# Expert layers that fetch token rows by indirect reads and send results by indirect writes

## What is computed

```python
probs = softmax(x2 @ wr)                       # x2: normalized tokens
gate_v, gate_i = top_k(probs, TOP_K)
pos = place of the token among those that chose the same expert
keep = pos < C
buf[ef, posc] = tok * keep                     # one block of C rows per expert
h = gelu(einsum('ech,ehf->ecf', buf, w1) + b1)
y = einsum('ecf,efh->ech', h, w2) + b2
out = x + sum over choices of y[ef, posc] * gate * keep
```

| layer | experts | choices per token | rows per expert | hidden width |
|---|---|---|---|---|
| A (L0) | 64 | 2 | 78 at most | 256 |
| B (L2) | 8 | 1 | no limit, in blocks of 250 | 512 |
| C (L3) | 8 | 2 | 250 at most | 256 |

## Time and profile before

### The profile page before, as it was taken

The page is one execution under the profiler, slowest core; times in us unless marked ns, Lnnn a source line. Parts: engine busy times, 40 slices in busy tenths (PEclk is TensorE's granted clock), DMA queues, the critical chain, the costliest instruction groups (busy, mean ns, idle before and its releaser), DMA issues. The chain is left out here.

```text
span 3491.5 us, 42084 instructions
## 1 busy us (share of the span) xinstructions
PE 2712.7 (78%) x12559; PEld 1905.1 (55%) x12560; DVE 1672.9 (48%) x3338; ACT 944.3 (27%) x2087; POOL 245.7 (7%) x247
## 2 busy tenths in 40 slices
PE   5888869967999872999488599946868589998554
PEld 3555546446878642666265266645635367775442
DVE  6777742154888532443433632231132378884323
ACT  1222230112777610111111122211111247774100
POOL 0000000000000103111200000010010000000123
PEclk9999989988999875999698799958979789998576
DMA  7000060211000015997323120014341100000354
GB/s 250 24 0 0 0 170 2 57 42 29 18 21 14 16 33 185 305 314 257 99 51 122 38 58 12 1 66 156 107 102 27 52 25 22 21 15 8 84 165 119
DMA packets 133922, 269.43 MB, mean 77 GB/s; under 512 B 44950, under 2 KB 46182, under 8 KB 132539
## 3 DMA queue, kind: packets, MB, share of 16 engines
q10 hardware_dynamic: 53198, 116.25, 11.2%
q1 hardware_dynamic: 51245, 106.69, 10.0%
q0 software_dynamic: 29376, 45.16, 4.3%
HBM read 189.78 MB, written 73.05 MB: 75 GB/s over the span
## 5 line engine op out<-in xcount | busy, mean ns | idle before, releaser
L1042 DVE TENSOR_REDUCE mx<-ps 125x1 f32<-125x500 f32 (+1 forms) x480 | 274.3, 589 | 57.6 <-PE ps L812 41.0
L243 PE MATMUL ps<-onehot_src,onehot_dst 125*128 x1200 | 258.7, 354 | 42.2 <-DVE onehot_dst L219 17.5
L937 ACT ACTIVATE probs_hi<-ps 125x500 fp32r<-125x500 f32 (+1 forms) x480 | 255.4, 532 | 125.5 <-DVE probs_lo L994 81.1
L218 DVE TENSOR_SCALAR onehot_src<-iota,src_f 125x1250 f16 x400 | 217.6, 544 | 112.4 <-PE ps L243 100.0
L939 ACT ACTIVATE x<-ps 125x500 f32<-125x500 f32 (+1 forms) x480 | 258.7, 539 | 0.0
L994 DVE TENSOR_TENSOR probs_lo<-x,probs_hi 125x1250 fp32r<-125x1250 f32 x160 | 240.9, 1506 | 34.9 <-ACT x L939 31.4
L1525 DVE COPY yb<-ps 78x512 f32<-78x512 f32 (+1 forms) x100 | 68.7, 688 | 349.4 <-PE ps L1462 220.9
L1462 PE MATMUL ps<-w2s,hT 128*78 128x512 f32 (+1 forms) x480 | 217.1, 599 | 2.7 <-ACT hT L1487 2.6
L243 PEld LDWEIGHTS ps<-onehot_src,onehot_dst 125*128 x1200 | 120.8, 102 | 173.6 <-issue 119.7
L1487 ACT ACTIVATE hT<-ps,b1s 128x78 f32<-128x78 f32 (+1 forms) x240 | 66.6, 342 | 519.7 <-PE ps L1453 495.9
L812 PE MATMUL ps<-K_hi_lo,Q_hi_twice 128*125 128x500 f32 (+1 forms) x480 | 182.5, 386 | 22.2 <-DVE mx L1042 16.9
(11 more groups left out here) (346 smaller groups left out, 4869.2 us busy)
## 6 DMA issues: line engine op xcount, KB each, us to landing
room<-in_L_ffn_w_p ACTq DMA_DIRECT2D x72, 512.0 KB, 7.1
w2s<-in_L_ffn_w ACTq DMA_DIRECT2D x72, 512.0 KB, 7.3
buf<-zeros SPq DMA_DIRECT2D x37, 512.0 KB
G<-c_spill ACTq DMA_DIRECT2D x2, 5859.4 KB
xb<-buf SPq DMA_DIRECT2D x64, 156.0 KB
yb<-yb POOLq DMA_DIRECT2D x64, 156.0 KB, 7.0
xb<-buf SPq DMA_DIRECT2D x36, 250.0 KB
tv<-in_L_ffn_tv_W_p SPq DMA_DIRECT2D x2, 4096.0 KB
```

Of the source, the lines that this page charges most:

```text
L218: v.tensor_scalar(ohs[:, slot, :].rearrange("p o n -> p (o n)"), io16[:, 0:N], sF[:, bass.ds(tile, 1)], None, ALU.is_equal)
L243: mm_ = pe.matmul(ps[:, 3 * half + c, 0:cn], ohd[:, slot, :].rearrange("p o n -> p (o n)"), ohs[:, slot, c0:c0 + cn].rearrange("p o n -> p ...
L937: act.activation(PH[:, t % 2, c0:c0 + cn], ps[0:P, ST + n, 0:cn], ACT.Exp, scale=SCALE).then_inc(p_hi, 1)
L1042: v.tensor_reduce(mx[:, t, n:n + 1], ps[0:P, SQ + cc % 2, 0:cn], AX.X, ALU.max)\
```

## The change

Routing now forms, for each slot of each unit, the number of the token that fills it (`take`) and the row to which its result goes (`give`, numbered by choice and token; unused slots read token 0 and write to spare rows). It does so with one-hot matrices and one chain of products on PE. In the same block SP writes the normalized token rows, dense, to HBM, and ACT issues all first-layer biases and the weights of the first three groups. In `experts` POOL gathers the rows of each unit by indirect DMAs and scatters its results by indirect DMAs; SP's loop of loads is gone. In A and C `xb` and `yb` hold two units (`DEEP`); in B one. The second bias and the residual are added to `x` at the start of `experts`. `combine` loads the results with direct DMAs from SP and ACT, in five parts, and in A and B takes the row statistics that the next stage needs. The start of the program fills fewer rows of HBM with zeros. The diff, cut to its core (of `combine`, `program` and the table of `route` only added lines; layer A takes the branch `NB == E_`):

```diff
--- before.py
+++ after.py
+            @block.sync
+            def _(sp):
+                for to, what in in_two(rowtiles(r.rows_dram), rows_in):
+                    sp.dma_start(to, what).then_inc(r.rows_out, 16)
+                sp.wait_ge(r.rows_out, 32)
...
+                for n in range(topk * T):
+                    c, t = n // T, n % T
+                    pe.wait_ge(hots, 2 * c + 2)
+                    mm = pe.matmul(ps[0:R, 1, 0:NB], rowhot[:, c, t, :], unithot[:, c, t, :], start=(n == 0),
+                                   stop=(n == topk * T - 1))
+                mm.then_inc(slots_done, 1)
...
+                if early is not None:
+                    early(act)
...
+                def rows_of_slots(c, row):
+                    v.tensor_tensor(rowhot[:, c, :, :], ioR[:, :].unsqueeze(1).broadcast_to([P, T, R]),
+                                    row.unsqueeze(2).broadcast_to([P, T, R]), ALU.is_equal).then_inc(hots, 1)
+                def units_of_slots(c, out, hot, number):
+                    return v.tensor_tensor(out, hot, number.unsqueeze(2).broadcast_to([P, T, hot.shape[2]]), ALU.mult)
...
+                    if NB == E_:
+                        for c in range(2):
+                            rows_of_slots(c, pk[:, c, :])
+                            units_of_slots(c, unithot[:, c, :, :], OH[:, c, :, :], token1[:, c, :]).then_inc(hots, 1)
...
+                v.wait_ge(slots_done, 1)
+                s.did(v.tensor_copy(slots[0:R, 0, :], ps[0:R, 1, 0:NB]))
+                s.wait()
+                s.did(v.tensor_scalar(slots[0:R, 1, :], slots[0:R, 0, :], float(N), -float(N), ALU.is_gt, ALU.mult))
+                s.wait()
+                s.did(v.tensor_tensor(slots[0:R, 1, :], slots[0:R, 1, :], slots[0:R, 0, :], ALU.add))
+                s.did(v.scalar_tensor_tensor(slots[0:R, 2, :], slots[0:R, 0, :], 0.5, no_row[0:R, :], ALU.is_lt, ALU.mult))
+                s.wait()
+                s.did(v.tensor_scalar(r.take[:, :], slots[0:R, 1, :], -1.0, 0.0, ALU.add, ALU.max))
+                s.did(v.scalar_tensor_tensor(r.give[:, :], slots[0:R, 0, :], -1.0, slots[0:R, 2, :], ALU.add, ALU.add))
...
+    def issue_first(self, act):
+        act.dma_start(self.b1s[:, :, :], self.b1).then_inc(self.w_in[0], 16)
+        for g in range(self.RING - 1):
+            self.issue(act, 0, g)
...
-        xb = sb("xb", [R, 2, D])
+        xb = sb("xb", [R, DEEP, 2, D])
         xbT = sb("xbT", [128, 2, 2, C, R])
         hT = sb("hT", [128, 2, FC, R])
-        yb = sb("yb", [R, 2, D])
-        put_done = k.gpsimd_dma_semaphore(nc, "put_done")
+        yb = sb("yb", [R, DEEP, 2, D])
...
-                def rows(i, u, g):
-                    for s in range(2):
-                        sp.wait_ge(turned[s], u + 1)
-                        sp.dma_start(xb[:, s, :], buf[rows_of(u, s), :]).then_inc(rows_loaded[s], 16)
-                sp.wait_ge(put_done, 16 * r.topk * T)
-                run(sp, rows)
...
+                def gather(u, slot):
+                    for s, rows in enumerate(slots_of(r.take, 0, u)):
+                        pool.indirect_dma_start(xb[:, slot, s, :], None, r.rows_dram,
+                                                bass.IndirectOffsetOnAxis(ap=rows, axis=0))\
+                            .then_inc(rows_loaded[slot][s], 16)
+                def scatter(u, slot):
+                    for s in range(2 if dynamic else 0):
                         pool.wait_ge(y_out[s], u + 2)
-                        pool.dma_start(ybuf[rows_of(u, s), :], yb[:, s, :]).then_inc(stored[s], 16)
+                    for s, rows in enumerate(slots_of(r.give, 1, u)):
+                        if not dynamic:
+                            pool.wait_ge(y_out[s], u + 2)
+                        pool.indirect_dma_start(y_dram, bass.IndirectOffsetOnAxis(ap=rows, axis=0),
+                                                yb[:, slot, s, :], None).then_inc(stored[s], 16)
+                def landed(u):
                     for s in range(2):
                         pool.wait_ge(stored[s], u * 16 + 16)
                         pool.sem_inc(yb_free[s], 1)
-                run(pool, store)
+                def emptied(u):
+                    for s in range(2):
+                        pool.wait_ge(turned[s], u + 2)
...
+                pool.wait_ge(r.rows_out, 32)
+                for s in range(2):
+                    pool.sem_inc(yb_free[s], DEEP)
+                gather(0, 0)
+                if dynamic:
+                    units = pool.snap(pool.value_load(r.tab[0:1, 2, 0:1], min_val=wts.E_, max_val=r.max_blocks))
+                    with pool.Fori(0, units - 1) as u:
+                        emptied(u)
+                        gather(u + 1, 0)
+                        scatter(u, 0)
+                        landed(u)
+                    scatter(units - 1, 0)
+                    landed(units - 1)
+                else:
+                    gather(1, 1)
+                    for u in range(UNITS):
+                        if u + 2 < UNITS:
+                            emptied(u)
+                            gather(u + 2, u % 2)
+                        scatter(u, u % 2)
+                        landed(u)
...
+                for t in range(T):
+                    if t >= 2:
+                        pe.wait_ge(bias_taken, t - 1)
+                    pe.matmul(ps[0:P, BIAS[t % 2], :], r.gateT[:, P * t:P * t + P], b2, start=True, stop=True)\
+                        .then_inc(bias_summed, 1)
...
-                        pe.wait_ge(rows_loaded[s], u * 16 + 16)
+                        pe.wait_ge(rows_loaded[parity][s], nth * 16)
...
+                for t in range(T):
+                    v.wait_ge(bias_summed, t + 1)
+                    v.tensor_tensor(x[:, t, :], x[:, t, :], ps[0:P, BIAS[t % 2], :], ALU.add).then_inc(bias_taken, 1)
+                if res is not None:
+                    v.wait_ge(bias_taken, T)
+                    v.tensor_tensor(x[:, :, :], x[:, :, :], res[:, :, :], ALU.add)
...
+def combine(nc, k, r, x, y_dram, out=None):
     with ExitStack() as ctx:
+        K_, HALVES = r.topk, 5
+        n = T // HALVES
+        Y = ctx.enter_context(nc.sbuf_tensor(k.name("Y"), [P, K_, T, D], fp32))
+        got = [ctx.enter_context(k.semaphore(nc, k.name("got"))) for _ in range(HALVES)]
+        added, stored = (ctx.enter_context(k.semaphore(nc, k.name(s))) for s in ("added", "stored"))
         with nc.Block() as block:
+            def loads(eng, c):
+                src = rowtiles(y_dram[c * N:c * N + N, :])
+                for h in range(HALVES):
+                    for to, what in in_two(Y[:, c, n * h:n * h + n, :], src[:, n * h:n * h + n, :]):
+                        eng.dma_start(to, what).then_inc(got[h], 16)
+            @block.sync
+            def _(sp):
+                loads(sp, 0)
+                if out is not None:
                     for t in range(T):
+                        sp.wait_ge(added, K_ * (t + 1))
                         sp.dma_start(out[P * t:P * t + P, :], x[:, t, :]).then_inc(stored, 16)
                     sp.wait_ge(stored, 16 * T)
+            if K_ == 2:
+                @block.scalar
+                def _(act):
+                    loads(act, 1)
             @block.vector
             def _(v):
                 for t in range(T):
+                    v.wait_ge(got[t // n], 32 * K_)
                     for c in range(K_):
+                        if c:
+                            v.wait_ge(added, t * K_ + c)
+                        v.scalar_tensor_tensor(x[:, t, :], Y[:, c, t, :], r.gate[:, c, t:t + 1], x[:, t, :],
+                                               ALU.mult, ALU.add).then_inc(added, 1)
+                    if out is None and t:
+                        v.wait_ge(added, t * K_)
+                        v.bn_stats(k.stats[:, t - 1, :], x[:, t - 1, :])
+                if out is None:
+                    v.wait_ge(added, T * K_)
+                    v.bn_stats(k.stats[:, T - 1, :], x[:, T - 1, :])
...
+                for r0 in range(0, 2 * N, 250):
+                    sp.dma_start(y_dram[r0:r0 + 250, :].rearrange("(p q) n -> p q n", q=2),
+                                 zeros[0:P, :].rearrange("p (q n) -> p q n", q=2)).then_inc(start_done, 16)
+                    n += 16
                 sp.wait_ge(start_done, n)
```

More of the change, by code:

```diff
@@ L1257, in _ @@
                         s.did(v.tensor_scalar(keep[:, c, :], pk[:, c, :], float(cap), None, ALU.is_lt))
[L1258 to L1273, removed]
                     s.wait()
@@ L1356, in group @@
                 body(i, e, g)
[L1358 to L1363, removed]
         def run_ahead(eng, ahead, body, after=None):
@@ L1371, in both @@
                 def both(i, u, g):
-                    ahead(u, 0, True)
+                    ahead(u, u + 1, 0, True)
                     body(i, u, g, 0)
-                run(eng, both, after)
+                with eng.Fori(0, ROUNDS) as i:
```

(47 more changed lines are left out.)

245 lines of the change are left out of this document (134 added, 111 removed).

## The result

The changed kernel takes 3638.9 us (median of 4; 3636.2 to 3641.1) against 3491.4 for the one before (4 runs): a ratio of 1.042, 95% interval 1.040 to 1.044. It is slower, as forecast, but by more than twice as much: 147 us instead of 67 (3556 was forecast, with a range up to 3615). The profiled execution has a span of 3637.2, 145.7 more than before.

What follows compares the result with a forecast made beforehand. Units were taken as paced by PE, a store's round trip close behind. A +102, B -12.5 and C -22.5, together +67, gave 3560, or 3556 on the median's footing; 8-in-10 range 3435 to 3615.

Steps and rivals of the forecast that it cites:

- The fill: Expert block's start until the first unit's last product: -26 us in layer A, -20 in B, -25 in C.
- the routing: Routing block of each expert layer: added products and steps cost +8 us each in A, B and C.
- A's combine: Layer A's combine block: direct loads, then DVE products and statistics, 28.5 us against 39.7 + 6.03: -17.
- E(0): End of PE's last product in unit 0 of an expert block: 38.4 us instead of 64.1 in A.
- The chain of A's units: Layer A's units: POOL's landing wait delays gathers; two steps 25.9 us, 31 steps 403 against 269.1: +134.
- L: Landing of a result scatter in the units, meeting the weights' burst: 7.5 us, bounds 5.2 and 9.8.
- L': Landing of the second row gather in the units: 5.5 us from old combine gathers, bounds 5.2 and 6.8.
- c: Clock loss while PE restarts from a stall, per two unit steps: 2.4 us, from nothing to 3.3.
- The second rival: Indirect DMAs of 78 rows land like direct ones, 2.2 to 2.7 plus 0.6 us: 3406 us; chance 0.12.
- The first: Scatter and gather land outside weight bursts, 5.2 us each, no clock loss: about 3465 us; chance 0.20.
- The third: Full contention in the units: scatter landing 9.8, gather landing 6.8, clock loss 3.3 us: 3624 us; chance 0.15.
- The forecast of C's combine: Layer C's combine block: loads and stores bound it, about 29.5 us against 53.1: -23.5.

Runs made afterwards that it cites:

- the seventh experiment: Kernel with both POOL order edits (gather one unit earlier, wait for the scatter before), bias moved behind the units, residual behind the first scaling: 3384.9 us.
- experiments 1 to 3: Changed kernel with the gather queued one unit earlier, 3458.2 us; with POOL waiting for the scatter before, 3511.8; with both edits, 3415.2.
- experiment 6: Changed kernel with the weights reloaded inside A's and C's units cut to 128 x 32 elements for each DMA: 3465.6 us.
- experiments 2 and 4: Changed kernel with POOL waiting for the scatter before, 3511.8 us; changed kernel with seven extra PE products before every second unit's transposes, 3657.5.
- experiment 10: Changed kernel with each indirect read and write in C moving 120 rows instead of 125: 3623.5 us.
- experiment 2: Changed kernel with POOL waiting for the scatter of the unit before instead of the one just issued: 3511.8 us.
- experiment 5: Changed kernel with nine and two extra PE products ahead of the two halves of every second unit's transposes: 3686.7 us.
- experiment 7: Kernel with both POOL order edits, bias products moved behind the last unit and residual sum behind the first unit's scaling: 3384.9 us.

## Why the prediction was right or wrong

**The fill, the routing, the block ends, A's combine, B** were within 4 us each, by the steps given. (The terms given for A's combine, 5.8, 15 and 6, add up to 26.8 and not to 28.5; the block took 30.6.) E(0) came 39.8 us after the barrier (38.4 forecast), behind bias products of 17.40 at the same low clock. What the sum didn't ask is whether the bias needs to stand there: the seventh experiment takes another 30 us out.

**The chain of A's units** is the one described: PE's transposes wait for the gather, the gather for POOL's wait, POOL for its store. The claim that the second buffers don't help because the wait is in POOL's program order was right too, and experiments 1 to 3, which change POOL's order and waits alone, show it. What failed are the sizes of two terms. In the pair shown:

- L, forecast 7.5 and 0.4 more for semaphores, took 7.4 with them (1372.14 to 1379.57): right.
- **L', forecast 5.5, took 7.9** (1380.85 to 1388.71), above its bound of 6.8. The step that failed is "L': old combine gathers". Those ran beside little. This gather starts the moment PE has drained the next group, when ACT issues the next weights (1379.53); it meets a burst just as the scatter did. Where the weights are cut away (experiment 6), gathers land in 3.2.
- **c, forecast 2.4, took 5.3**, above its bound of 3.3. The bound counted w1's loss (7.04 against 3.74) and not w2, which runs slow too: 7.03 + 5.49 and the transposes are 12.9 to E(2) against 7.6. The row of the fill that gave the 7.04 has a slow w2 beside it, 4.35. A wait of 2 us was enough for much of it (experiments 2 and 4). Windows of the changed kernel, the unit before the wait and w1 behind it, with the granted clock at 1.00 and at 0.50:

```profile
1371.50:1379.30 7.80, 7.76 (x48) 5.21 (x48) 3.24 (x10) 1.20 (x4) 0.94 (x1) 1.00 0.89 308
1389.20:1396.00 6.80, 6.80 (x35) 6.80 (x34) 1.16 (x4) 0.54 (x2) 1.94 (x2) 0.50 0.19 61
```

These two add 2.4 and 2.9, and the other terms came out 0.7 lower together: 25.9 becomes 30.5. In C, where +15 became +21.7, the forecast gave its step of about 12 without a sum. There the scatter is the long one, 9.0 us with its semaphores in the first pair (3495.34 to 3504.33), the second gather takes some 5, and w1 alone is slow:

```profile
3495.34 1.20 POOL L1526 DMA_INDIRECT expert_rows<-yb,give  x1 [0.50 <-DVE yb L1654]
...
3504.33 1.23 POOL L1516 DMA_INDIRECT xb<-rows,take  x1 [7.79 <-DMA expert_rows<-yb,give]
...
3512.35 5.55 PE L1592 MATMUL ps<-xbT,room 128*128 128x125 f32 x32
```

**The bounds' foundation was off even where the value held.** 5.2 was taken as the least for any indirect transfer. It is the price of 125 rows; 78 rows land in 2.8 to 3.2 without weights (experiment 6). The second rival's premise, that rows of A land like direct ones, was thus true of the transfer alone, and with its times the serial order costs nothing (8.55 a step). It did not happen because the weights' burst falls on both transfers. The Trainium skill's rule quoted in the prediction ("DMA: Bandwidth & Descriptors", section on the anatomy of a DMA on the GpSimd path; an estimate of 2.4 us for 160 KB) is near these 2.8 to 3.2. Its estimate for 250 KB, 2.6, is half of what 125 rows take.

**Rivals.** The first (landing outside the bursts, no loss of clock) fell on both counts. The third, 3624, came nearest, by other terms: not a slower scatter, but L' and the clock beyond their bounds.

**The forecast of C's combine** failed at "loads and stores bound it, about 29.5": the block took 45.2. The bandwidth was taken as the loads' own, but the ten stores of 125 rows moved 127 GB/s at a DMA share of 0.33, and 17 us of them were left behind the last sum. Split, they lost 11.5 us. The Trainium skill ("DMA: Bandwidth & Descriptors", section "Why a DMA increments its semaphore by 16 and not by 1") says that a transfer goes to the largest number of engines, up to 16, that divides the outermost counts of both its sides. The trace agrees as far as its DMA share goes: the rule gives 5 engines for 125 rows, 5 of 16 is 0.31, and 0.33 was measured; 120 rows would have 15. No run splits the stores into two halves, so what a second store in flight gives by itself isn't shown. That indirect transfers follow the same rule is in line with experiment 10, but no row here counts their engines.

**Left open:** 7.2 us between the layers and 3 us of C's routing. The code between the layers is all but the same; the stretches from A to B and from B to C take 576.4 to 580.0 and 665.9 to 669.6 us in the changed kernel and those made from it, so some of the 7.2 can be scatter.

## What to carry to other kernels

A queue that both fetches and stores shouldn't wait for the landing of what it has just issued while a later unit's fetch stands behind the wait, when landings are long: fetch a unit earlier and wait for the store before, and the buffers that are there begin to count. Price a transfer from rows that run beside the same burst and have the same number of rows, and add to each wait of PE the slow products behind it, which can cost more than the wait. Look at the DMA share of a stretch that is bound by transfers: a third, as here, can mean that few engines carry it.

## What the runs showed of the hardware

- PE's granted clock falls after short waits: 1.94 and 0.40 us ahead of a clock of 0.59 and 3.3 us lost (experiment 2). It can fall after less. In the kernel of experiment 5, behind a wait of 0.72, the window 1530 to 1556 has PE busy for 25.79 of 26 us at a granted clock of 0.56, that is for most of it the lower level of 1.2 GHz, and the nine extra products (18 instructions) take 13.07 instead of 7.96. Two of the fifteen long steps are such (30.0 us each); the cause is open. The windows before it and of it:

```profile
1503.00:1530.00 27.00, 25.81 (x119) 14.38 (x118) 7.76 (x21) 2.17 (x8) 7.95 (x9) 1.00 0.64 209
1530.00:1556.00 26.00, 25.79 (x64) 14.32 (x65) 2.53 (x9) 2.37 (x5) 5.54 (x6) 0.56 0.36 118
```

- 120 rows land faster than 125: 3.7 to 3.9 us against 5.5 to 6.0, both beside weights.
- An indirect transfer's issue on POOL takes 5.35 us while DVE runs the residual sum of 5.48, against 0.96 (experiment 7), as in the earlier trace rows.
